# Routing moved into the cross attention, and the experts' work cut into four equal chunks, in a two-layer decoder kernel

## The reference, cut to what matters

```
x = x + _L1_xattn_ref(_layernorm(x), ctx_1024, ...)      # 16 heads of 8, 77 keys
x = x + _L1_ffn_ref(_layernorm(x), ...)                  # experts

scores = sigmoid(x @ gate_w.T) + gate_bias               # T = 4096 tokens, E = 64 experts
group_scores = scores.reshape(T, 8, 8).max(-1)           # 8 groups of experts, the best 4 are kept
masked_scores = scores * mask
topk_w, topk_i = top_k(masked_scores, 6)                 # 6 experts a token
topk_w = topk_w / (topk_w.sum(-1) + 1e-08)
h = silu(x @ eg_w.T) * (x @ eu_w.T)                      # 64 hidden channels per expert
out = shared(x) + sum over the 6 experts of topk_w * (h @ ed_w.T)
```

## Time and profile before

| | us |
|---|---|
| median of 3 runs | 1998.6 (1994.36 to 2005.5) |
| the profiled execution | 2002.38 |
| its span | 2000.6 |
| TensorE busy | 1713.8 (86%) |
| VectorE busy | 1342.0 (67%) |
| ScalarE busy | 1223.9 (61%) |
| GpSimd busy | 942.7 (47%) |
| mean TensorE clock granted | 0.929 of 2.4 GHz |

### The profile page before, as it was taken

One profiled execution on the slowest core, in us unless ns is written; L12 is line 12 of the kernel. 1 busy time (PEld: TensorE's weight loads), 2 busy tenths in 40 slices (PEclk: granted clock), 3 DMA queues, 4 the chain that ended last, 5 costly groups with the idle time before them and its releaser, 6 DMA issues.

```text
span 2000.6 us, 46446 instructions
## 1 busy us (share of the span) xinstructions
PE 1713.8 (86%) x15613; PEld 1436.5 (72%) x15613; DVE 1342.0 (67%) x3995; ACT 1223.9 (61%) x2893; POOL 942.7 (47%) x1220
## 2 busy tenths in 40 slices
PE   6999999999999999998328999999974759896863
PEld 4877778888888888875127787878753759895842
DVE  4667767777766666656887778766678576475543
ACT  3666567776777777765873666787742636563520
POOL 2555544444444444430002655522107777777776
PEclk7999999999999999999759999999976989998986
DMA  6533497000000000000003344456613537675632
GB/s 180 170 113 114 131 348 237 2 2 2 2 2 2 2 2 2 2 1 1 0 0 111 100 123 130 118 152 184 176 30 107 184 134 269 214 259 180 200 110 73
DMA packets 156593, 208.47 MB, mean 104 GB/s; under 512 B 19069, under 2 KB 125757, under 8 KB 156221
## 3 DMA queue, kind: packets, MB, share of 16 engines
q1 hardware_dynamic: 137916, 175.54, 28.2%
q0 software_dynamic: 12288, 25.19, 4.1%
q10 hardware_dynamic: 6160, 4.78, 0.7%
HBM read 96.74 MB, written 108.95 MB: 103 GB/s over the span
## 4 chain that ended last, share of the span: by engine, by line
PE 65%; POOL 9%; DVE 9%; issue 6%; ACT 4%; SPq 3%; DMA 3%; ACTq 0%; POOLq 0%; DVEq 0%
POOL yk L2493 7%; PE bank L1000 6%; PE score_banks L285 6%; PE bank L1016 6%; PE score_banks L989 5%; PE bank L941 5%; PE bank L942 4%; PE bank L943 4%; PE bank L296 4%; PE score_banks L2000 3%; PE score_banks L267 3%; PE bank L1986 2%; SPq L202 2%; PE score_banks L266 1%; PE score_banks L2016 1%
## 5 line engine op out<-in xcount | busy, mean ns | idle before, releaser
L1439 POOL TENSOR_TENSOR pw<-ew,rw 128x410 f32<-128x410 f32 x256 | 222.5, 869 | 369.3 <-DVE rw L1289 369.3
L465 ACT ACTIVATE pt<-score_banks 128x512 f32<-128x512 f32 (+1 forms) x384 | 229.7, 600 | 115.6 <-PE score_banks L285 115.0
L1153 ACT ACTIVATE ew<-score_banks,nmax 128x205 f32<-128x205 f32 x512 | 217.4, 434 | 103.2 <-DVE nmax L1282 101.9
L579 DVE TENSOR_REDUCE nmx<-score_banks 128x4 fp32r<-128x512 f32 (+1 forms) x288 | 171.6, 596 | 123.1 <-PE score_banks L267 120.1
L731 POOL TENSOR_SCALAR_AFFINE_SELECT pt<-pt 128x512 f32<-128x512 f32 x256 | 164.6, 644 | 167.1 <-ACT pt L465 167.0
L285 PE MATMUL score_banks<-q_pack,k_diag 128*128 128x128 f32 (+1 forms) x1536 | 238.4, 279 | 0.4
L2481 POOL DMA_INDIRECT slots_in<-xh,idx x192 | 189.7, 988 | 88.5 <-issue 57.6
L285 PEld LDWEIGHTS score_banks<-q_pack,k_diag 128*128 128x128 f32 (+1 forms) x1536 | 189.8, 181 | 46.3 <-issue 37.1
L2493 POOL DMA_INDIRECT yk<-slots_out,idx x192 | 183.5, 956 | 58.5 <-issue 57.6
L267 PE MATMUL score_banks<-k_diag,q_pack 96*128 96x512 f32 (+1 forms) x384 | 187.9, 491 | 1.2 <-DVE nmx L575 0.7
L1162 ACT COPY pwt<-bank 128x512 f32<-128x512 f32 x256 | 150.1, 586 | 46.9 <-PE bank L1000 46.9
(11 more groups left out here) (396 smaller groups left out, 4375.3 us busy)
## 6 DMA issues: line engine op xcount, KB each, us to landing
xr<-slots_in SPq DMA_DIRECT2D x56, 512.0 KB
slots_out<-yr SPq DMA_DIRECT2D x56, 512.0 KB, 3.1
slots_in<-zero SPq DMA_DIRECT2D x2, 8704.0 KB, 51.2
q_rows<-q_hi SPq DMA_DIRECT2D x96, 128.0 KB, 2.9
q_pack<-q_rows SPq DMA_DIRECT2D x32, 384.0 KB
slots_in<-zero SPq DMA_DIRECT2D x2, 5632.0 KB, 33.5
experts<-in_experts SPq DMA_DIRECT2D x25, 320.0 KB, 3.8
q_rows<-q_lo SPq DMA_DIRECT2D x48, 128.0 KB, 3.0
```

What stands on the lines that cost most here:

```text
L465: nc.scalar.activation(m.pt[0:a.keys, c, :, :].rearrange("p h t -> p (h t)"), m.flip[c % 2][0:a.keys, :], ACT.Exp).then_inc(s.exped.semaph ...
L579: nc.vector.tensor_reduce(m.nmx[:, b % 2, :, 0, c], m.score[c % 2][:, 0:HC * a.columns].rearrange("p (h k) -> p h k", h=HC)[:, :, 0:a.keys ...
L1153: last = nc.scalar.activation(m.ew[:, n % 2, h, :], score_bank(m, n, h), ACT.Exp, bias=m.nmax[:, n // 2, 2 * (n % 2) + h:2 * (n % 2) + h + 1],
L1439: nc.gpsimd.tensor_tensor(m.pw[:, n, :, :], m.ew[:, n % 2, :, :], m.rw[:, n % 2, :].unsqueeze(2).broadcast_to([128, 2, KW]), ALU.mult)\
```

## The change

1. **Chunks.** `SPANS` becomes (0, 2), (2, 4), (4, 6), (6, 8): 4 chunks of two groups, 14 rounds each, still 56 rounds.
2. **Routing inside the cross attention.** Groups 0 and 1 are normalised (on GpSimd), transposed, routed and ranked from sequence 5 to 19, with the starts, list and slots of chunk 0; groups 2 and 3 are routed from sequence 20 to 31. One step a slot instead of two. The reciprocal of 1 + exp is in four parts, one a slot; adding 1 and adding the bias are on GpSimd. TensorE waits at fixed places for ScalarE's copy and exponentials (`before_maxima`) and for `rank` (`before_inputs`).
3. **Early scatters.** 40 of the 48 scatters of chunk 0 stand in the cross attention on GpSimd, four a sequence from sequence 21 to 30.
4. **One step less.** `route` has 15 steps; the weights are normalised in `shares` (one operation there takes the reciprocal sum in as well).
5. **Lists and slots of chunks 2 and 3** move from between the rounds into rounds 8, 9, 11 and 12.
6. **Combines.** Combine 0 is in round 43, and one follows in every second round.
7. SyncE waits for the last update of the cross attention before its first load. Several small tiles lie in other places; some semaphores are shared.

```
-SPANS = (0, 1), (1, 4), (4, 7), (7, 8)
+SPANS = (0, 2), (2, 4), (4, 6), (6, 8)
...
+EARLY_SCATTERS = 40
...
     def after(n):                                   # moe_tensor
-        if n == 1:
+        if n == 0:
+            table(1)
+        elif n == 1:
             transpose_inputs(4)
...
+        if n == AHEAD + 5:
+            table(2)
+        elif n == AHEAD + 8:
+            table(3)
...
     def tail(b, c):                                 # moe_tensor
-        if (b, c) == (27, 0):
-            transpose_inputs(0)
-        if (b, c) == (28, 0):
-            logits(0)
-        if (b, c) == (31, 1):
-            ranks(0)
+        if (b, c) in ((7, 2), (11, 2)):
+            wait(pe, cross.values, b + 9)
+            transpose_inputs((b - 7) // 4)
+        elif (b, c) in ((8, 2), (12, 2)):
+            logits((b - 8) // 4)
+        elif (b, c) in ((13, 3), (17, 3)):
+            wait(pe, cross.keys, b + 9)
+            ranks((b - 13) // 4)
...
+        elif (b, c) == (28, 3):
+            ranks(2)
+
+    def before_maxima(b):
+        if b in (7, 11, 22):
+            pe.wait_ge(s.x_f, {7: 1, 11: 2, 22: 3}[b])
+        elif b in (8, 12, 23):
+            pe.wait_ge(s.scores, {8: 1, 12: 2, 23: 3}[b])
...
     def after(n):                                   # moe_vector
...
+        if n == AHEAD + 6:
+            for g in (4, 5):
+                spread_slots(g)
+                slots(g)
+        elif n == AHEAD + 9:
+            for g in (6, 7):
+                spread_slots(g)
+                slots(g)
...
+        if n in (AHEAD + 5, AHEAD + 8):
+            starts(2 + (n - AHEAD) // 8)
+            list_tiles(2 + (n - AHEAD) // 8)
+            keep_table(2 + (n - AHEAD) // 8)
+        if 0 <= n - FIRST_OF[1] < B:
             shares(n - FIRST_OF[1])
-        if 0 <= n - FIRST_OF[2] < 16:
-            shares(16 + n - FIRST_OF[2])
-        if 0 <= n - FIRST_OF[2] - 6:
-            combine(n - FIRST_OF[2] - 6)
+        if n > FIRST_OF[3] and (n - FIRST_OF[3]) % 2 == 1:
+            combine((n - FIRST_OF[3]) // 2)
...
+        if 41 <= i < 55:                            # moe_vector, tail, i = 4 * b + c
+            route(0, 1 + i - 41)
+        elif 57 <= i < 71:
+            route(1, 1 + i - 57)
+        elif 101 <= i < 115:
+            route(2, 1 + i - 101)
+        elif 115 <= i < 128:
+            route(3, 1 + i - 115)
...
+    def early(b, k):                                # moe_pool
+
+        if b < 21:
+            return None
+        n = 4 * (b - 21) + k
+        return n if n < EARLY_SCATTERS else None
```

More of the change, by code:

```diff
@@ L738, in body @@
             widen_values(*place(a, b + 1), u + 1)
+        if between is not None:
+            between(b, 0)
         if a.causal:
@@ L744, in body @@
             query_lows(*place(a, b - 1 + a.ahead))
+        if between is not None:
+            between(b, 1)
         if a.causal:
@@ L748, in body @@
             key_lows(*place(a, b - 1 + a.ahead))
+        if between is not None:
+            between(b, 2)
         if a.causal:
@@ L754, in body @@
             add_base(*place(a, b + 1 + a.ahead))
+        if between is not None:
+            between(b, 3)
         if fill_later is not None:
@@ L2189, in run @@
     def run():
-        for g in range(1, 4):
-            copy_inputs(g)
-            routing_scores(g)
         for n in range(NR):
@@ L2204, in moe_vector, with normalise @@
 def moe_vector(dve, nc, m, s, cross, link):
-    def normalise(g):
-        for q in range(GB):
+    def normalise(g, part):
+        for q in part:
             b = GB * g + q
@@ L2218, in route @@
     def route(g, n):
-        at = ROUTE_STEPS * g + n
+        at = routed(g, n)
+        if g < INSIDE and n == 1:
+            dve.wait_ge(s.biased, g + 1)
         wait(dve, m.s.route, at)
+        if n == 8 and g == 3:
+            wait(dve, cross.packed, 48 * B)
         if n == 0:
@@ L2298, in starts @@
         link(nc.vector.tensor_tensor(m.off[:], m.ends[:], m.n128[:], ALU.subtract))
+        wait(dve, s.started, chunk)
+        nc.vector.memset(m.tmp[:, 4:5], 0.0).then_inc(s.started, 1)
     def list_tiles(chunk):
@@ L2420, in run, with invert @@
-    def run():
-        normalise(1)
-        rank(0)
-        starts(0)
-        list_tiles(0)
-        slots(0)
-        for k in range(2):
-            nc.vector.memset(m.ht[F * (1 - k):F * (1 - k) + F, k, :], 0.0)
-        normalise(2)
-        normalise(3)
-        keep_table(0)
-        for n in range(ROUTE_STEPS):
-            route(1, n)
-        for g in (2, 3):
-            for n in range(ROUTE_STEPS):
-                if n == 4:
-                    rank(g - 1)
-                route(g, n)
+    def invert(g, q):
+        dve.wait_ge(s.lifted, g + 1)
+        part = m.sg[:, E * q:E * q + E]
+        nc.vector.reciprocal(part, part).then_inc(s.inverted, 1)
@@ new lines, in norm_steps @@
+    def norm_steps(at, measured, first):
+        wait(dve, cross.measured, measured)
+        for i in range(first, min(first + 2, NORM_STEPS)):
+            norm_alone(nc, m, link, m.stats, m.rstd, m.shift, 128, at, i)
+        if first + 2 >= NORM_STEPS and at is not MIDDLE:
+            k = 2 + FOURTHS.index(at)
+            nc.vector.memset(m.tmp[:, k:k + 1], 0.0).then_inc(s.measured, 1)
+    def tail(b, c):
+        i = NC * b + c
+        if 21 <= i < 27:
+            norm_steps(FOURTHS[0], 4, 2 * (i - 21))
+        elif 37 <= i < 43:
+            norm_steps(FOURTHS[1], 8, 2 * (i - 37))
+        elif 81 <= i < 87:
+            norm_steps(MIDDLE, 16, 2 * (i - 81))
+        if b in (9, 13, 24, 27):
+            invert({9: 0, 13: 1, 24: 2, 27: 3}[b], c)
+        if 41 <= i < 55:
[6 more added lines that the diff above has]
+            route(3, 1 + i - 115)
+        if (b, c) in ((13, 3), (17, 3)):
+            rank((b - 13) // 4)
+        elif (b, c) == (18, 1):
+            starts(0)
+        elif (b, c) == (18, 2):
+            list_tiles(0)
+        elif (b, c) in ((19, 1), (19, 3)):
+            dve.wait_ge(s.spread, 2 + 2 * (c // 3))
+            slots(c // 3)
+        elif (b, c) in ((21, 3), (22, 0)):
+            normalise(2, (range(2, 4), None, None, range(0, 2))[c])
+        elif (b, c) in ((22, 3), (23, 0)):
+            normalise(3, (range(2, 4), None, None, range(0, 2))[c])
+        elif (b, c) == (29, 0):
+            rank(2)
@@ L2438, in run @@
+    def run():
+        route(3, ROUTE_STEPS - 1)
+        keep_table(0)
         rank(3)
@@ L2497, in run, with moe_sync @@
     def run():
-        pool.wait_ge(s.blanked, 16 * len(SPANS))
-        for g in range(G):
-            scatter(g)
+        for n in range(EARLY_SCATTERS, B * EK):
+            scatter(n)
         for b in range(B):
             gather(b)
-    return run
-def moe_sync(sp, m, s, out, x_view):
+    return between, run
+def moe_sync(sp, m, s, cross, out, x_view):
     def load(n):
@@ L2529, in store_result @@
             .then_inc(m.s.stored, 16)
+    wait(sp, cross.updated, B)
     for chunk in range(len(SPANS)):
```

309 lines of the change are left out of this document (170 added, 139 removed).

## The result

The changed kernel takes 2073.4 us (median of 4 runs, 2062.0 to 2083.7) where the kernel before takes 1996.5 in the same comparison: ratio 1.0354, 95% interval 1.0309 to 1.0399, slower. The forecast was 2047 with a range of 2014 to 2068, so the sign and the mechanism of the tail held and the size was 26 us short. The profiled execution took 2072.8 for a span of 2071.0. Its mean granted clock was 0.912; the other three runs had 2083.7, 2074.0 and 2062.0 us at 0.904, 0.910 and 0.920: from run to run the time goes with TensorE's clock.

What follows compares the result with a forecast made beforehand. TensorE was taken to bound the cross attention and GpSimd's scatters and gathers the experts before the change. After it, gate 55 at 1865.8 plus a tail of 183.2 gave a span of 2049.0, so 2047 us, range 2014 to 2068.

Steps and rivals of the forecast that it cites:

- The new wait: Expert part: gathers wait for VectorE's later combines to free four buffers; 21 gather sequences, 158.8 us, stand behind round 55.
- step 7: Expert part, from gate 55 to the end: gather 11 starts at +16.3, then 158.8 and 8.1, 183.2 us in all.
- the check from GpSimd's side: GpSimd behind the cross attention: 25 us lost before scatter 96 and 64 before combine 0, against 62 saved.
- near 1720: Sign for the first gather on GpSimd, in the expert part: it should start near 1720 us.
- T: End of the cross attention, 1490.05 us in the kernel before; forecast at 1502.
- steps 3 to 6: Expert rounds: gate 8 at T + 69.6, gate 14 at T + 137.7, gate 42 at 1800.4, gate 55 at 1865.8 us.
- step 1: Cross attention: inserted TensorE work, new waits and VectorE routing lengthen it by 12 us, bounds 0 and +30.
- step 2: Start of the experts: VectorE's remaining routing delays product 0 to T + 11.2 instead of T + 8.9, so +2.3 us.
- Slow scatters in the cross attention: Rival: early scatters take 1.64 us each beside busy VectorE, cross attention ends at T + 26, time 2073; chance 0.05.
- GpSimd stays the bound: Rival, expert part: VectorE's combines keep up, time about 1945; chance 0.06, together with anything below 1989.

Runs made afterwards that it cites:

- before_late: Kernel before with only the changed kernel's combine rule (combine 0 in round 43, then every second round, 7 inside the rounds): 2066.6 us, ratio 1.0294.
- paced_b: Changed kernel with combines 0 to 18 at chosen places from round 31 on, two of them between rounds 41 and 42, second run: 1992.4 us, ratio 0.9929.
- pe_twice: Changed kernel with TensorE's transposes and logits of groups 0 to 3 issued twice: ratio 1.0011 on a held-up chip.
- two_of_three_b: Changed kernel with combines from round 34 on in two of three rounds, 15 inside the rounds, second run: 2019.4 us, ratio 1.0064.
- no_early: Changed kernel with 0 instead of 40 scatters inside the cross attention, all 192 behind it: ratio 1.0089 on a held-up chip.

## Why the prediction was right, and where it was short

- **The new wait and the tail** (step 7, the check from GpSimd's side): right in mechanism and size. Hole 68.4 us for 64, tail 180.3 for 183.2, 321 between the gathers for 320; `before_late` and `paced_b` show that the rule makes it, in either kernel. The hole came out so close because both of its ends are late by about the same: the 24th gather ends at 1770.7 for 1750 and combine 0 at 1838.8 for 1814. The first gather, 1740.5, missed the sign "near 1720" by 20 us: T is 16 later, and the wait for the row numbers of group 4 is 30.45 for 25. The check from GpSimd's side also left out the waits behind the hole, for combines that come only in every second round: 12.9 us (81.3 less 68.4).
- **The rounds** (steps 3 to 6). Gates 0 to 8 take 65.5 us for 64.1. Gates 8 to 13 take 49.2 for 48.8, and 13 to 14 20.0 for 3.4 + 15.9. Chunks 1 and 2 take 160.6 for 160.6, chunk 3 to gate 55 67.4 for 65.4.
- **The cross attention** (step 1) is the term that was mis-sized: +28 for +12, near the edge of its bounds of 0 and +30. That TensorE's own work counts in full was right, as `pe_twice` shows for A. The new waits that I priced at 3 us are not those that came: TensorE shows none for the copies and exponentials of the routing, and what counts is TensorE standing for `o` behind VectorE's steps, 11.0 us in all where the kernel before has 3.3, with 3.1 more for ScalarE's `ot`. I priced VectorE by the length of a sequence, 5 us less 2.5, with one small step in each slot, where two steps of the normalisation and a whole list of row numbers (2.4 us) stand in one slot. And I left out the clock, which the earlier trace rows showed at 1.00: A and C hold 10 and 34 us at 1.2 GHz, worth about 3 and 17 us by the comparison of equal code above (half of the time at the low level; an estimate for C).
- **Gate 0** (step 2): T + 10.0 for T + 5.5. "Loads of the first chunk can start at T itself" was wrong. Only 40 of the 48 scatters of chunk 0 are placed inside, and the other 8 stand behind them; the last runs from 1520.29 to 1521.25, 3.1 us behind T, and the load at 1522.58 waits for it. In `two_of_three_b`, where the 48th scatter ends at 1517.25 and T is 1519.67, the load starts at 1519.33 and gate 0 comes at T + 5.0: the 5.5 was right for scatters that are done.
- **Rivals.** Slow scatters in the cross attention: its time of 2073 is what was measured, for another reason; the scatters take 0.96 to 1.30 us there, and `no_early` shows that they cost the stage nothing. The exclusive lock of the port, for which I had named the Trainium skill (Trainium Architecture — The Big Picture, What this means for kernel authors), leaves no mark in these rows. GpSimd stays the bound: false for this change, true behind T once the combines are in place (`paced_b`). Even there the time is 1992 and not 1945: T is 15 us later than that rival took it, and it left out the wait for the row numbers of group 4, 29.7 us there. So the change as a whole did pay with its combines in place, by less than that rival had.
- **The range** ended at 2068, 5 us short: it took +25 of the cross attention's +30 and no spread between runs, which is 22 us here and goes with the clock. That the median lies so near the edge is the cross attention's 16 us of miss; the other terms missed by 6 together.

## What to carry to other kernels

A consumer that frees buffers is part of the producer's chain: when a change moves work earlier, ask when each buffer comes free and not only when the work could start. Fill gaps of a side engine only behind what the bound engine waits for, and look at the slot in which the filler stands, not at its sum. Where TensorE is the bound, price a new wait by its length and by the stretch at 1.2 GHz that may follow it.
